# A macaron transformer layer on 8 cores: each tile's second layernorm directly behind its FFN product, in the main rounds

## What is computed

```python
x = x + 0.5 * ffn(layernorm(x), rhs)
x = x + attn(layernorm(x), Wq, Wk, Wv, Wgk1, Wgk2, bgk2, Wg, gnw, Wo)
x = x + 0.5 * ffn(layernorm(x), rhs)

def ffn(lhs, rhs):           # int8 quantisation of rows and columns
    lhs_scale = max(|lhs|, over a row) / 127
    rhs_scale = max(|rhs|, over a column) / 127
    return (round(lhs / lhs_scale) @ round(rhs / rhs_scale)) * lhs_scale * rhs_scale

def attn(x, ...):            # gated linear attention, 16 heads, dk 32, dv 64
    q, k, v, g = x @ Wq, x @ Wk, x @ Wv, x @ Wg
    gk = log_sigmoid(x @ Wgk1 @ Wgk2 + bgk2) / 16
    h = h * exp(gk) + k v^T ; o = q h      # a scan over the rows
    return (rmsnorm(o) * gnw * silu(g)) @ Wo
```

## Time and profile before

| | us |
|---|---|
| median of the two runs shown | 3151.07 (3077.88 and 3224.26) |
| profiled execution | 3080.43 |
| its span, slowest core (core 5) | 3078.9 |
| spans of the 8 cores | 3060.6 to 3078.9 |
| PE busy | 1594.6 (52%) |
| DVE busy | 1061.9 (34%) |
| ACT busy | 514.8 (17%) |
| POOL busy | 477.0 (15%) |
| mean granted TensorE clock, core 5 | 0.761 of full speed |

### The profile page before, as it was taken

The page is one execution under the profiler, slowest core; times in us unless marked ns, Lnnn a source line. Parts: engine busy times, 40 slices in busy tenths (PEclk is TensorE's granted clock), DMA queues, the critical chain, the costliest instruction groups (busy, mean ns, idle before and its releaser), DMA issues.

```text
span 3078.9 us, 25121 instructions; the slowest of 8 cores (3060.6 to 3078.9 us)
## 1 busy us (share of the span) xinstructions
PE 1594.6 (52%) x7218; PEld 870.9 (28%) x7218; DVE 1061.9 (34%) x2471; ACT 514.8 (17%) x1117; POOL 477.0 (15%) x979
## 2 busy tenths in 40 slices
PE   1101444534575476547654755575466547645654
PEld 1000212222333143224322332433143224323332
DVE  2613142324324432442343143324432432342053
ACT  0011112121211121111112121212121111212021
POOL 0003453001011102201210131012102201310120
PEclk9998666666787777768776877787778768776867
DMA  2433432112130213023101311230213013111310
GB/s 57 138 126 123 151 123 103 41 48 62 55 110 0 69 55 109 28 69 110 55 28 41 110 55 34 87 112 1 69 55 109 28 41 110 55 34 50 107 43 14
DMA packets 104456, 216.73 MB, mean 70 GB/s; under 512 B 16480, under 2 KB 41072, under 8 KB 104320
## 3 DMA queue, kind: packets, MB, share of 16 engines
q1 hardware_dynamic: 71072, 107.10, 10.6%
q0 software_dynamic: 28928, 92.30, 9.1%
q10 hardware_dynamic: 4320, 15.73, 1.6%
HBM read 189.89 MB, written 25.17 MB: 70 GB/s over the span
## 4 chain that ended last, share of the span: by engine, by line
PE 47%; DVE 17%; ACT 7%; issue 7%; DMA 5%; DVEq 4%; POOL 1%; SPq 1%; ACTq 0%; POOLq 0%
PE PF L502 14%; PE PF L770 6%; PE PP L480 4%; PE PF L395 4%; DVEq L141 4%; PE PA L480 3%; DMA WH<-wgh 2%; DVE YSC L739 2%; PE PA L646 2%; PE PO L395 2%; PE PP L523 2%; PE PO L672 2%; DVE U2TL L436 2%; PE PT L427 2%; ACT U2TH L433 2%
## 5 line engine op out<-in xcount | busy, mean ns | idle before, releaser
L385 PE MATMUL PT<-IDFB,T1SC 128*128 128x128 bf16 x176 | 25.7, 300 | 507.8 <-DVE T1SC L372 489.7
L502 PE MATMUL PF<-WH,U2TH 128*128 128x512 bf16 x608 | 174.6, 439 | 215.4 <-DMA WH<-wgh 97.7
L603 DVE TENSOR_TENSOR KHT<-KT,EXX 128x128 f32<-128x128 f32 x80 | 24.8, 312 | 535.1 <-ACT EXX L599 534.6
L461 POOL DMA_DIRECT2D WL<-wvl x64 | 33.9, 537 | 883.6 <-PE PA L480 883.4
L427 PE MATMUL PT<-IDF,YSC 128*128 128x128 f32 x176 | 47.8, 427 | 229.5 <-ACT YSC L421 160.0
L385 PEld LDWEIGHTS PT<-IDFB,T1SC 128*128 128x128 bf16 x176 | 15.3, 126 | 524.8 <-issue 524.8
L502 PE MATMUL PF<-WL,U2TH 128*128 128x512 bf16 x608 | 153.4, 398 | 0.4 <-DMA WL<-wgl 0.4
L502 PEld LDWEIGHTS PF<-WH,U2TH 128*128 128x128 bf16 x608 | 62.8, 108 | 311.7 <-issue 262.4
L631 POOL TENSOR_TENSOR QX<-QTE,QMASK 128x128 f32<-128x128 f32 x256 | 103.6, 438 | 292.0 <-DVE QTE L625 292.0
L502 PE MATMUL PF<-WH,U2TL 128*128 128x512 bf16 x608 | 143.6, 379 | 0.0
L395 PE MATMUL PF<-QFFN,UQT 128*128 128x512 bf16 x352 | 130.4, 550 | 0.0
(11 more groups left out here) (213 smaller groups left out, 3320.6 us busy)
## 6 DMA issues: line engine op xcount, KB each, us to landing
WH<-wvh SPq DMA_DIRECT2D x88, 256.0 KB, 4.1
WL<-wvl POOLq DMA_DIRECT2D x64, 256.0 KB, 5.1
WL<-wgl POOLq DMA_DIRECT2D x64, 256.0 KB, 6.8
WH<-wgh SPq DMA_DIRECT2D x64, 256.0 KB, 9.3
WL<-wol POOLq DMA_DIRECT2D x64, 256.0 KB, 7.0
WH<-woh SPq DMA_DIRECT2D x64, 256.0 KB, 9.5
XR<-x ACTq DMA_DIRECT2D x22, 512.0 KB, 8.0
WH<-wkh SPq DMA_DIRECT2D x88, 128.0 KB, 2.8
```

The lines of the kernel that those rows point to most:

```text
L461: b.step(loq, lambda e, dt=dt, nw=nw, lo_d=lo_d, cb=cb: e.dma_start(WL[:, cb + dt * nw:cb + (dt + 1) * nw], lo_d[dt * 128:(dt + 1) * 128, :]),
L502: la=(ci == 2 and dt == 7): e.matmul(PF[:, nb * 512:(nb + 1) * 512], xop[:, dt * R + i * 128: dt * R + (i + 1) * 128], wop[:, dt * D + nb ...
```

## The change

In the main rounds the loop over the two tiles that applies the FFN now also does the tile's second layernorm and its transposes, so that tile 0 is carried to U2TH and U2TL before tile 1's FFN product is written. In the prologue the two loops stay as they were: `if pro` with the FFN, then `if pro` again with the layernorm.

```diff
         if pro:
             for tile, key in res:
                 emit_ffn(tile, key)
+        if pro:
+            for il, (tile, key) in enumerate(res):
+                emit_ln2_u2t(tile, key, il)
         else:
             quant_next(rnd - n_pro_rounds, rnd)
             for il, (tile, key) in enumerate(res):
                 emit_ffn_apply(tile, key, FQB(il), slc=(18 + il, f"stq{il}"),
                                altp=True)
-        for il, (tile, key) in enumerate(res):
-            emit_ln2_u2t(tile, key, il)
+                emit_ln2_u2t(tile, key, il)
```

## The result

The changed kernel takes 1.0096 times as long as before, 95% interval 1.0078 to 1.0114. On 3088 us, the mean of the nine executions of before that took less than 3100 us, that is 29.6 us more, 24 to 35. The sum of the prediction was 34.0 us more. The medians over all runs are 3090.28 us before (10 runs) and 3121.39 after (11 runs). The two profiled executions took 3080.43 and 3115.82, 35.4 apart; that of before was one of its quicker ones. As some executions of a kernel are several per cent longer, with a lower clock on the cores of one die, the ratios leave those out.

A forecast was written before the change was run, and what follows sets the result against it. No engine is full; waits between DVE, ACT and PE at eight main round starts bound it. Legs of 30.78 + 6.42 = 37.20 us, 4.25 more each, give 34.0 on 3080.43: 3114.4 us; kernel's range 3088 to 3130, up to 3195 for the median.

The forecast's parts named there:

- E0 to T0: Tile 0's product with ABC (L401) to its first L427 transpose: L401, L404, statistics, YSC; 6.93 us.
- T0 to tile 1's second L385: Tile 0's first L427 transpose, through ACT's eight casts and the UQT copy, to tile 1's second L385 block; 8.81 us.
- from there to E1 (x): Tile 1's second L385 block to its L401, across its FFN product at 1.2 GHz; 6.42 us, 4.16 before.
- E1 to T1: Tile 1's L401 to its first layernorm transpose, same instructions as before for tile 1; 6.93 us.
- E0 to G: Round's start, tile 0's L401 to emit_gk's first matmul (L523); 37.20 us against 32.95, 4.25 more a round.
- ACT leg: Tile 0's first transpose to tile 1's second L385: UQT copy waits for ACT's eighth cast to end; 8.81 us.
- two legs with statistics: Each tile's L401 to its first layernorm transpose, with L401, L404, statistics and YSC; 6.93 us each.
- term of 0.52 for ACT's queue: Tile 1's UQT copy behind ACT's casts for tile 0; 8.81 against 8.29, 0.52 us more a round.
- step on the median: Whole kernel: median 3151.07 stood 71 above the profiled execution through one long run; a similar median would give 3187.
- warm product: Tile 1's FFN product: PE's clock doesn't fall or comes back first; x = 4.16, 3096 us; chance 0.08.
- free of PE's order: Tile 1's product runs during tile 0's statistics, not held by PE; 2.59 us less a round, 3060 us; chance 0.01.
- The third: Projections behind emit_gk's first matmul stay longer at 1.2 GHz; slower by over 2%, 3143 us and up; chance 0.07.

The follow-up runs named there:

- uqt_first: Against the changed kernel, tile 1's transposes and two UQT copies go ahead of tile 0's layernorm, its product staying behind tile 0's transposes; 0.998 of before.
- overlap_late: Against the changed kernel, tile 1's transposes and product go ahead of tile 0's layernorm, tile 1's L401 and L404 behind tile 0's split; 0.994 of before.
- fill: Changed kernel's order plus 58, 24 and 22 unread matmuls in PE's pauses between tile 0's product and tile 1's; 0.9998 of before.
- half: The new order in main rounds 1, 3, 5 and 7 only, the old order in the others; 1.0053 of before.

## Why the prediction was right and wrong

**The mechanism held, leg by leg.** PE's list keeps tile 1's product behind tile 0's transposes, and ACT's list keeps its copies behind the casts (uqt_first takes the second away, overlap_late both, and that turns the loss into a gain with the layernorm just as early). The product then starts at the lower clock (fill). The loss is per round (half).

| leg | predicted | core 4 after |
|---|---|---|
| E0 to T0 | 6.93 | 7.12 to 7.13 in seven rounds, 7.42 in one |
| T0 to tile 1's second L385 | 8.81 | 8.60 or 8.61 |
| from there to E1 (x) | 6.42 | 5.42 to 6.72, mean 6.23 |
| E1 to T1 | 6.93 | 7.21 to 7.40 |
| T1 to G | 8.11 | 8.11 to 8.40 |
| E0 to G | 37.20 | 36.67 to 37.89, mean 37.42 |

The busy time of the PO products was to be about 78 us and was 77.7.

**Small terms that were off.** The ACT leg was 0.2 too long, since the UQT copy starts 0.16 us after the start of the last cast, before that has ended, where I had let it wait for its end. The two legs with statistics were 0.2 and 0.3 too short. L307 starts 1.37 us after L404 now (1360.57 to 1361.94). Before it was 1.21, from L404 at 1354.17 to this row, where L404 belonged to tile 1 and L307 to tile 0:

```profile
1355.38 0.69 DVE L307 BATCH_NORM_STATS2 BN<-XR 128x6 f32<-128x512 f32 x1
```

 The builder puts a drain ahead of a DVE step that reads what an undrained earlier one wrote. In the new order L307 reads the XR that L404 has just written. That this is the cause of 0.16 of it is read from the trace and the builder's code, and was not tried by itself.

**The term of 0.52 for ACT's queue was rightly small as a difference, but misleading as a cause.** I gave it the difference to the old length of tile 0's split, 8.81 against 8.29. Taken away by itself (uqt_first), the place of the two copies is worth the whole loss, 4.4 us a round: PE can then start the product under the second half of the split, 3.9 us earlier, and the clock rises earlier in it, 0.5. Terms of a difference between two paths don't say what each would save alone.

**What failed is the step on the median.** I took the sum, 3114.4, from the profiled execution (3080.43), and held that the median shown, 3151.07, stood 71 us above it only because one of two runs was long. That was so: over ten runs the median is 3090.28, and 3121.39 after. But I left the forecast at 3114 beside a base of 3151, where it reads as a gain of 1.2%, while the argument says a loss of 1.1%, and the measurement says a loss of 0.96%. The 71 us belonged on both sides or on neither; the change should have been stated as a difference to one base. And I took 2% for about what a measurement can tell; this one tells 0.2%, so a loss of 1.1% should have been called a small loss, and not put under "no change". The range, up to 3195 for the sake of a second long run, was wider than the mechanism needed: 3121.39 lies in the kernel's own range, 3088 to 3130.

**The rivals.** A warm product didn't come: the clock was 0.50 in every window from 1364 until near the product's end. The product wasn't free of PE's order either. The third, a longer low clock behind G, would have put the loss beyond 60 us, against 35 at the upper end of the interval. The clock went the other way. Over the 64 round starts of the eight cores it leaves 0.50 at 5.0 us behind G before the change and at 3.7 after, and on every core the group with WGK1L is shorter (means 18.3 and 14.1 us in the run) and that with WL into PP too (46.9 and 43.4). I had put this at nothing, with 8 us either way in the range; it goes with the 4.8 us by which the stretches from G to E0 are shorter. So it is partly luck that the sum, 34.0, came so near the measured 29.6: E0 to G by itself gave 36.0. Why the clock rises earlier there wasn't tried. The slowest cores of the two profiled executions hide this, being 35.3 us apart.

## What to carry to other kernels

When each engine works its list in order, moving a tile's dependent chain forward also moves every engine's share of it, and an engine with other work to do meanwhile (here PE with the product, ACT with the copies that feed it) is blocked by its first waiting instruction. Move the parts that wait for nobody (statistics on DVE) and leave the independent product and its copies ahead of the instruction that waits: here it cost 1% when the whole function moved, and gave 1.3% and 2.2% when it was cut engine by engine. Look first at what each engine's list holds behind an instruction that waits; only then count what can lie beside what.

## What was not expected of the hardware

- Two DVE steps in a row (L404, L307) start 1.21 us apart when the second doesn't read the first, and 1.37 when it does and the engine drains between, as read from the timelines of before and after.
- Four float32 transposes of 128x128 took 1.09 us after a pause of PE of 7.2 us and 0.63 us after one of 2.15 us or after fillers; the clock is part of the price of transposes too.
- 104 matmuls that nobody reads, in each of eight rounds, made the changed kernel faster (0.9998 against 1.0096 of before). The legs of DVE and ACT kept their length: E0 to T0 is 7.13 us with and without them.
